# Moving a per-token middle stage into the window loop of a two-layer attention kernel, with the key split and the ones moved to other engines

## The reference, cut to what matters

```python
# layer 0: linear attention (ReLU features), mixed over tokens by a plain reshape
q, k, v = LN(x @ wq), LN(ctx @ wk), LN(ctx @ wv)
kv = einsum('bhnd,bhne->bhde', relu(k) + eps, v)
att = relu(q) @ kv / (relu(q) @ sum(k))
# the middle stage: all of it works on one token at a time
x = x + tanh(g_xattn[0]) * LN(att.reshape(B, -1, 128) @ dense_w + dense_b)
xq = round(LN(x) * 127 / max|LN(x)|)               # 8-bit rows, ternary weights
h = silu(xq @ w_gate) * (xq @ w_up)                # 128 -> 512
x = x + tanh(g_ffn[0]) * (round(h * 127 / max|h|) @ w_down)
q1 = LN(x) @ W_q                                   # queries of layer 1
# layer 1: softmax attention over the context, then 8 experts, 2 of them per token
s = softmax(q1 @ (ctx @ W_k).T / sqrt(8)) @ (ctx @ W_v)
x = x + tanh(g_xattn[1]) * (s @ W_o);  x = x + tanh(g_ffn[1]) * moe(LN(x))
```

## Time and profile before

| | us |
|---|---|
| time before, median of 3 runs | 834.42 (831.93 to 837.05) |
| the profiled execution, own time | 833.69 |
| its span | 831.8 |
| TensorE busy | 701.4 (84%) |
| VectorE busy | 563.2 (68%) |
| ScalarE busy | 482.8 (58%) |
| GpSimd busy | 252.7 (30%) |

### The profile page before, as it was taken

One profiled execution on the slowest core, in us unless ns is written; L12 is line 12 of the kernel. 1 busy time (PEld: TensorE's weight loads), 2 busy tenths in 40 slices (PEclk: granted clock), 3 DMA queues, 4 the chain that ended last, 5 costly groups with the idle time before them and its releaser, 6 DMA issues.

```text
span 831.8 us, 19578 instructions
## 1 busy us (share of the span) xinstructions
PE 701.4 (84%) x7276; PEld 485.1 (58%) x7277; DVE 563.2 (68%) x1099; ACT 482.8 (58%) x718; POOL 252.7 (30%) x236
## 2 busy tenths in 40 slices
PE   0599989985436489999999999999999999699997
PEld 0477767773313145666656666566665666467786
DVE  7699999984778767776767668676777775420111
ACT  0377777770324227667776777767777677344431
POOL 8198888880103522022210222112220110000000
PEclk9899999996657669999999999999999999699999
DMA  3022223344600071675446644466445561101110
GB/s 129 15 98 75 74 74 101 101 139 20 136 0 1 6 160 44 152 159 110 104 101 156 156 100 101 111 156 156 90 102 120 119 135 39 45 16 51 51 37 24
DMA packets 59460, 74.16 MB, mean 89 GB/s; under 512 B 35309, under 2 KB 40167, under 8 KB 59423
## 3 DMA queue, kind: packets, MB, share of 16 engines
q1 hardware_dynamic: 59422, 73.65, 37.3%
HBM read 32.61 MB, written 1.40 MB: 41 GB/s over the span
## 4 chain that ended last, share of the span: by engine, by line
PE 57%; DVE 24%; issue 10%; ACT 3%; DMA 1%; SPq 1%; POOL 1%; DVEq 1%; ACTq 0%
DVE mx L1227 8%; PE ps L605 7%; PE ps L496 7%; PE ps L663 6%; PE ps L675 6%; PE ps L488 6%; PE ps L592 6%; PE ps L482 5%; PE ps L431 3%; DVE ss L1029 3%; PE ps L445 2%; PE ps L517 2%; DVE xn L981 2%; ACT arena L735 2%; DVE arena L1049 2%
## 5 line engine op out<-in xcount | busy, mean ns | idle before, releaser
L1227 DVE TENSOR_REDUCE mx<-ps 128x1 f32<-128x500 f32 x336 | 214.3, 674 | 88.6 <-PE ps L496 87.4
L829 ACT ACTIVATE P<-ps,kbias,kscale 125x896 f32<-125x896 f32 x192 | 210.5, 1098 | 76.0 <-PE ps L592 71.7
L922 POOL TENSOR_TENSOR KP<-kvall,KP 128x1500 bf16<-128x1500 f32 x16 | 48.6, 3035 | 317.4 <-ACT KP L785 317.4
L496 PE MATMUL ps<-KP,Qb 128*128 128x500 bf16 x336 | 131.9, 394 | 9.8 <-issue 4.4
L605 PE MATMUL ps<-P,Vp 125*32 125x112 f32 x3072 | 113.4, 265 | 1.8 <-ACT P L829 1.3
L431 PE MATMUL ps<-wkv,cT 128*125 128x256 f32 x384 | 91.6, 382 | 1.2 <-ACT arena L748 1.2
L605 PEld LDWEIGHTS ps<-P,Vp 125*32 125x32 f32 x3072 | 67.1, 109 | 39.3 <-issue 31.5
L431 PEld LDWEIGHTS ps<-wkv,cT 128*125 128x125 f32 x384 | 69.1, 189 | 10.2 <-issue 1.5
L592 PEld LDWEIGHTS ps<-QS,KS 128*128 128x128 bf16 x768 | 53.9, 99 | 34.7 <-issue 18.5
L592 PE MATMUL ps<-QS,KS 128*128 128x112 bf16 x768 | 68.4, 214 | 5.7 <-DVE QS L1233 5.1
L592 PEld LDWEIGHTS ps<-QS,arena 128*128 128x128 bf16 x768 | 52.1, 98 | 33.3 <-issue 18.5
(11 more groups left out here) (190 smaller groups left out, 1000.6 us busy)
## 6 DMA issues: line engine op xcount, KB each, us to landing
cT<-ctxT_dram SPq DMA_DIRECT2D x32, 750.0 KB, 4.3
KS<-KP SPq DMA_DIRECT2D x48, 375.0 KB, 7.3
arena<-KP SPq DMA_DIRECT2D x48, 375.0 KB, 7.0
QS<-QD SPq DMA_DIRECT2D x96, 28.0 KB, 5.7
wgu<-w_dram SPq DMA_DIRECT2D x8, 256.0 KB, 2.8
...
```

The source lines that it names most:

```text
L496: ins = nc.tensor.matmul(ps[:, bank, 0:KCW], q[:, 128 * c:128 * c + 128], KP[par][0][:, KCW * k:KCW * k + KCW], start=True, stop=True)
L829: nc.scalar.activation(P[t % 2][0:TK, :].rearrange("p (k n) -> p k n", k=2), src, ACT.Exp, scale=kscale[0:TK, bass.ds(n, 1)], bias=kbias[0 ...
L1227: ins = v.tensor_reduce(mx[:, c, k:k + 1], ps[:, bank, 0:KCW], AX.X, ALU.max)
```

## The change

The middle stage no longer runs on all 8 tiles ahead of the windows. Tiles 0 and 1 still do, tile by tile; tile n = i+2 goes through it in the pair of windows i (windows 2i and 2i+1), for i = 0 to 5. Pairs 6 and 7 have no such work. Its products are ten new aux units (CHAIN): AT, DE (dense), XT, G (gate), U (up) in the first window of a pair, HT0, HT1, DN (down), LT, Q1 (query) in the second. PLACES becomes two tables. VectorE gets the per-tile steps between its maxima; GpSimd takes the inverse square roots (`deviation`: an add and a power of -0.5 on one column); SiLU is made of Tanh on ScalarE and a product on VectorE. Of the trip through DRAM, tiles 0 and 1 go first.

The key split: ScalarE writes the K unit in f32 to krest and frees the bank, then rounds krest to KP[0]; GpSimd subtracts KP[0] from krest; ScalarE rounds to KP[1] at the end of the window (t = 11; before t = 10); GpSimd makes KP[2] as before. `key_rest` is gone. The 1.0 in KS[0] and KS[1] are written by ScalarE (`fill_ones`, 6002 f32 that hold two bf16 ones each), at the very start and after the last step ahead of the windows.

```diff
-PLACES = [["MX0", "MX1", "V0"], ["MX2", "MX3", "MX4"], ["DEN", None, "V1"], ["MX5", "MX6", "V2"],
-          ["MX7", "WO", "K0"], ["MX8", "MX9", "MX10"], ["MX11", "MX12", "K1"], ["MX13", "MX14", "MX15"],
-          ["MX16", "MX17", "K2"], ["MX18", "MX19", "MX20"], [None, None, None], ["SH", None, None]]
-ALL = [u for places in PLACES for u in places if u]
+PLACES = [
+    [["MX0", "AT", "V0"], ["MX1", "MX2", "DE"], ["DEN", "MX3", "V1"], ["MX4", "MX5", "V2"],
+     ["MX6", "WO", "K0"], ["MX7", "MX8", "MX9"], ["MX10", "XT", "K1"], ["MX11", "MX12", "MX13"],
+     ["MX14", "MX15", "K2"], ["MX16", "MX17", "MX18"], ["MX19", "MX20", "G"], ["SH", None, "U"]],
+    [["MX0", "MX1", "V0"], ["MX2", "MX3", "MX4"], ["DEN", "HT0", "V1"], ["MX5", "HT1", "V2"],
+     ["MX6", "WO", "K0"], ["MX7", "DN", "MX8"], ["MX9", "MX10", "K1"], ["MX11", "MX12", "MX13"],
+     ["MX14", "LT", "K2"], ["MX15", "MX16", "MX17"], ["MX18", "MX19", "MX20"], ["SH", None, "Q1"]],
+]
+ALL = [[u for places in half for u in places if u] for half in PLACES]
 ENDS = ["DEN", "WO"]
-EARLY = ["K0", "K1", "K2", "V0", "V1", "V2", "K0'", "K1'", "K2'"]
-REST_LATER = 3
+CHAIN = ["AT", "DE", "XT", "G", "U", "HT0", "HT1", "DN", "LT", "Q1"]
...
+        KSF = [sb("KS0", [128, KSW // 2 + 1])[:], arena[:, 0:KSW // 2 + 1]]
+        KS = [k.bitcast(BF16)[:, 0:KSW] for k in KSF]
...
+            sp.wait_ge(sem("att0_ready"), 2)
+            mix_out(range(2, 5), "mix_out1")
+            sp.wait_ge(sem("mix_out0"), 64)
+            mix_in(slice(0, 2), "mix_in0")
+            mix_out(range(5, NT), "mix_out1")
+            sp.wait_ge(sem("mix_out1"), 32 * (NT - 2))
+            mix_in(slice(2, NT), "mix_in1")
...
+            for unit in EARLY_SIDE[0:3]:
+                fill(BEFORE, unit, 0, 0)
+            both("AT", "DE")
+            for unit in EARLY_SIDE[3:6]:
+                fill(BEFORE, unit, 0, 0)
+            both("XT", "G", "U")
+            fill(BEFORE, EARLY_SIDE[6], 1, 1)
+            both("HT0", "HT1", "DN")
+            fill(BEFORE, EARLY_SIDE[7], 1, 1)
+            both("LT")
+            fill(BEFORE, EARLY_SIDE[8], 1, 1)
+            both("Q1")
...
+            def fill_ones(n):
+                nc.scalar.copy(KSF[n], two_ones[:].broadcast_to([128, KSW // 2 + 1])).then_inc(sem(f"ks{n}_ready"), 1)
             act.wait_ge(sem("setup_done"), 1)
...
+            fill_ones(0)
...
+                if k == 0 and not (fixed(b) and b == 0):
+                    act.wait_ge(sem("kp3_ready"), b)
+                cols = slice(KCW * k, KCW * k + KCW)
+                nc.scalar.activation(krest[:, cols], ps[:, bank_of(at, unit), 0:KCW],
+                                     ACT.Identity, bias=bk_sb[:]).then_inc(sem("side_free"), 1)
+                act.wait_ge(sem("side_free"), emptied(at, unit))
+                nc.scalar.copy(KP[par][0][:, cols], krest[:, cols]).then_inc(sem("kp1_ready"), 1)
+            def key_part2(b, par):
+                act.wait_ge(sem("rest_ready"), b + 1)
                 nc.scalar.copy(KP[par][1][:], krest).then_inc(sem("kp2_ready"), 1)
...
+                elif unit == "G":
+                    act.wait_ge(sem("cg_ready"), n + 1)
+                    nc.scalar.activation(silu[:, z, :], ps[:, bank, :], ACT.Tanh,
+                                         scale=cg[:, z:z + 1]).then_inc(sem("tanh_ready"), 1)
...
+            key_part2(0, 0)
+            both("AT")
...
+            key_part2(1, 1)
+            act.wait_ge(sem("nd_ready"), 2)
+            fill_ones(1)
...
+                        if t == T - 1 and "K2" in has:
+                            key_part2(w + 2, par)
...
-                nc.gpsimd.memset(QS[n], 0.0)
-            nc.gpsimd.memset(KS[0], 1.0).then_inc(sem("zeroed"), 1)
...
+                pool.wait_ge(sem("kp1_ready"), KC * (b + 1))
+                nc.gpsimd.tensor_tensor(krest, krest, KP[par][0][:], ALU.subtract).then_inc(sem("rest_ready"), 1)
...
+            def deviation(n, j):
+                z = slot(n)
+                pool.wait_ge(sem("c_var"), turn(n, j, 3))
+                nc.gpsimd.tensor_tensor(sd[:, z:z + 1], mv[:, z, 1:2], (eps_ln if j else eps_in)[:], ALU.add).then_inc(sem("eps_added"), 1)
+                pool.wait_ge(sem("eps_added"), turn(n, j, 3))
+                nc.gpsimd.tensor_tensor(rstd[:, z:z + 1], sd[:, z:z + 1], mhalf[:], ALU.pow).then_inc(sem("rstd_ready"), 1)
...
-            nc.gpsimd.memset(KS[1], 1.0).then_inc(sem("ks1_ready"), 1)
...
+                    if par == 0 and chained:
+                        deviation(i + 2, 0)
+                        deviation(i + 2, 1)
+                    queries(b, par, i + 1, prev((i, par)))
+                    if par == 1 and chained:
+                        if not (fixed(i) and i == CHAIN_PAIRS - 1):
+                            mix_tile(i + 3)
+                        deviation(i + 2, 2)
...
+            def statistics(n, j, src):
+                z = slot(n)
+                v.bn_stats(stats[:, z, :], src).then_inc(sem("c_stat"), 1)
+                dve.wait_ge(sem("c_stat"), turn(n, j, 3))
+                pause()
+                v.bn_aggr(mv[:, z, :], stats[:, z, :]).then_inc(sem("c_var"), 1)
...
+            def dense(at, n):
+                z = slot(n)
+                name, = names(n, "DE")
+                src, free = opened(at, name)
+                v.tensor_tensor(lin[:, z, :], src, row[:, DENSE_B, :], ALU.add).then_inc(free, 1)
+                closed(at, name)
+                statistics(n, 0, lin[:, z, :])
+                dve.wait_ge(sem("c_var"), turn(n, 0, 3))
+                v.scalar_tensor_tensor(lin[:, z, :], lin[:, z, :], mv[:, z, 0:1], gmask[:], ALU.subtract,
+                                       ALU.mult).then_inc(sem("lin_ready"), 1)
...
+            def quantise(n):
+                z = slot(n)
+                dve.wait_ge(sem("rstd_ready"), turn(n, 1, 3))
+                v.tensor_scalar(nrm[:, z, :], x_of(n), mv[:, z, 0:1], rstd[:, z:z + 1], ALU.subtract,
+                                ALU.mult).then_inc(sem("n1_ready"), 1)
+                dve.wait_ge(sem("n1_ready"), n + 1)
+                row_steps(n, 0, nrm[:, z, :])
...
+            def gate(at, n):
+                z = slot(n)
+                name, = names(n, "G")
+                src, free = opened(at, name)
+                dve.wait_ge(sem("tanh_ready"), n + 1)
+                v.scalar_tensor_tensor(silu[:, z, :], silu[:, z, :], 1.0, src, ALU.add, ALU.mult).then_inc(free, 1)
...
+            def hidden_quantised(n):
+                z = slot(n)
+                dve.wait_ge(sem("qs_ready"), turn(n, 1, 2))
+                v.tensor_scalar(silu[:, z, :], silu[:, z, :], qs[:, z:z + 1], ROUND, ALU.mult,
+                                ALU.add).then_inc(sem("round_ready"), 1)
+                dve.wait_ge(sem("round_ready"), turn(n, 1, 2))
+                v.tensor_scalar(hqb[:, z, :], silu[:, z, :], ROUND, None, ALU.subtract).then_inc(sem("hq_ready"), 1)
+                v.tensor_scalar(cd[:, z:z + 1], cu[:, z:z + 1], wg2[:, 2:3], None,
+                                ALU.mult).then_inc(sem("cd_ready"), 1)
...
+                    elif unit == "DE":
+                        dense(at, n)
+                    elif unit == "G":
+                        gate(at, n)
+                    if chained:
+                        if unit == "MX5":
+                            first_sum(n)
+                        elif unit == "MX7":
+                            quantise(n)
+                        elif unit == "MX8":
+                            quantised(n)
...
+                if chained:
+                    hidden((i, 0), n)
...
+                        if unit == "MX0":
+                            hidden_steps((i, 0), n)
+                        elif unit == "MX1":
+                            hidden_quantised(n)
+                        elif unit == "MX10":
+                            normed(n)
```

742 lines of the change are left out of this document (429 added, 313 removed).

## The result

The changed kernel takes 857.55 us (median of 4 runs, 855.01 to 859.75) against 833.17 beside it (831.57 to 837.05). The ratio is 1.0286, 95% interval 1.0264 to 1.0308: slower, as forecast (850 us, range 808 to 864), and 7.5 us above the number. The profiled execution took 859.75 us (span 857.9), 26.1 more than the one of before; it is the longest of the four, and the clock differs among them (means of 0.914 to 0.930), so places where the clock falls are those of this execution.

The account below looks back on a forecast made before the run. Windows were taken as bound by TensorE's order, which waits for VectorE at a window's end. From 833.7 us, -6.5 (start), -41 (middle stage) and +63 (pairs) gave 849, stated as 850 against 834.4; range 808 to 864.

Parts of the forecast that it names:

- The start, -6.5: Kernel start: with the fill on ScalarE, the 8 normalisations run from 10.6 to 12.8, shifting everything behind by -6.5 us.
- The middle stage, -41: Between linear attention and first window: only 2 tiles go through ahead of the windows, -41 us, bounds -36 and -45.
- The hold that the forecast named as not isolated: Middle stage: dense's centring (L1348), with two SBUF inputs, would be held once by GpSimd reading SBUF, 1 us more.
- The first window, +5.0: First window of a pair: MX5, MX10 and XT wait for VectorE's steps, the gate for Tanh; +5.0 us.
- The second window, +2.7: Second window of a pair: hidden-row steps among MX0 to MX2 delay MX4, and the joint maximum comes late; +2.7 us.
- the port: Second window: VectorE's scaling and rounding wait for GpSimd's KP[2] and Qb; +2.7 us a pair, between 0 and 3.7.
- Rival 1: Pairs of windows: the port doesn't bite, a pair costs 7.7 us, total 833, no change; chance 0.24.
- Pair 0: First pair of windows: without DEN and WO it costs some 9 us, against 10.4 for a pair.
- its two bounds: Forecast's own range: port 1.5 to 3.7 us a pair, middle stage -36 to -45 us.
- Rival 3: Second windows: TensorE stands over 3 us at once, the clock falls, 2 to 3 us a pair more, 865; chance 0.12.
- Rival 2: Pairs: VectorE catches up, only TensorE's added products and the late gate stay, 4.3 us a pair, 812; chance 0.25.
- Rival 4: Windows: Tanh evicts Exp's table, two loads of 1.28 us a pair on ScalarE, 865; chance 0.01.

Follow-up runs that it names:

- e6: Changed kernel with GpSimd's KP[2] after the hidden rows' rounding, VectorE's quantisation one unit earlier and the gate's product at t = 8; 824.80 us, ratio 0.9897.
- e9: e6 plus Qb after the quantisation or rounding, KP[2] after Qb and On in the second window, dense's statistics behind MX3; 819.53 us, ratio 0.9828.
- e8: Changed kernel with 8 unread f32 products a pair that TensorE issues where it would wait; 847.39 us, ratio 1.0158.
- e1: Changed kernel, but in the first window's key part GpSimd starts KP[2] only after VectorE has scaled and rounded the hidden rows; 837.85 us, ratio 1.0047.
- e5: Changed kernel with the gate's product at t = 8, behind MX14, and MX15 to MX20 one or two places later; 862.36 us, ratio 1.0328.
- e3: Kernel before, with only the ones of both KS filled by ScalarE in place of GpSimd; 824.47 us, ratio 0.9892.
- e4: Kernel before, with only the key split: ScalarE writes f32 key rows and copies to bf16, GpSimd subtracts; 833.73 us, ratio 0.9998.

## Why the prediction was right, and where its numbers were off

**The start, -6.5: right, 1.4 short.** The step that failed is the table load behind the constants. There is one at 0.74, but it lies beside the setting of the constants, so the fill runs from 2.15 to 7.34 and not to 8.7. 5.19 us for 6002 elements is the rate taken from the 1500-element copy (5.3). By the Trainium skill (ScalarE: Activation LUTs, What ACT_TABLE_LOAD costs) a drain of some 1380 ns stands behind the load of a new set, and the forecast estimated a gain of 5.1 us from it. The rows show none: the load at 7.36 takes 1.28 and the square root runs at 8.65.

**The middle stage, -41: right.** First scores at 253.35 (forecast about 255). Of the -49.5, 7.2 had come by the products of L525 (L663 starts at 183.11 in place of 190.33), so the stage itself gave 42.3. AT is copied at 206.23; the forecast's 213.5 less 6.5 is 207.0. Qb ends at 235.9 and 238.6 (forecast 236.8). GpSimd's power had no row; it takes 0.55 for one column, the addition 0.19 to 0.24, so a root is 0.8 to 0.9 and not 0.6. The hold that the forecast named as not isolated is there: L1348 takes 1.32 beside KP[2] and 0.38 after it, 0.9 us. It has two inputs in SBUF. The Trainium skill (SBUF — State Buffer, Who interferes with whom) says that such an instruction contends with a GpSimd instruction that reads SBUF, and the trace agrees; L1509 in e6 (1.50 against 0.39 in e9) is a second case.

**The first window, +5.0: right at full clock.** Waits of 0.86, 0.91 and 0.84 us (forecast 1.05, 1.1 and 1.1) and of 1.65 in front of SH. e8 gives its length with the clock held up: 31.59 (forecast 31.25), +5.3. Windows without a fall in other runs agree: 31.67 in window 2 of after, 31.7 in window 4 of e1.

**The second window, +2.7 and +2.7 for the port: right, each 0.2 too dear.** The comparison is clean only at full clock. e6 without the hold: 28.76, +2.5. e8 with it: 31.27, so the port is 2.5 us. (e1's 29.18 has part of a fall in it; against that it would be 2.1.) At full clock the scaling took 1.74 (1.63 by the forecast), the rounding 1.79 (1.97); in after, where the second window starts at the lower clock, the scaling took 1.32. Rival 1, that the port doesn't bite, falls with these rows; e1 made it true and gave 837.9, near the 833 that this rival named, with the clock's falls still in it.

**The sum.** At full clock the middle pair takes 31.59 + 31.27 = 62.9, 10.4 over before, to the tenth what the forecast had; that it is the tenth is luck, since +0.3 in the first window and -0.2 twice in the second cancel. Pair 0 was priced at 9; in e8 it takes 62.2 against 51.6, so 10.7. Windows 12 to 14 cost 3.1 and not 2. With these the sum is 833.7 - 49.5 + 62.1 + 3.1 - 0.3 = 849, and e8, which is this with the clock kept up in the waits, took 847.4 (its first scores come 1 us sooner). That the sum is 849 again is luck in part too: 2.0 us were gained ahead of the windows and 2.2 lost in them. The forecast's own range of 843 to 858 is also narrower than its two bounds, which taken together give 839 to 861, and the measured 857.6 lies at its edge for a cause that was not in it.

**What failed is that the clock stood among the rivals and not in the sum.** Rival 3 said 2 to 3 us a pair and 865; it came at 1.8 (10.7 us over the six pairs) on top of all the rest, and that is the difference between 847 and 858. Its condition, a stand of over 3 us at once in a second window, held in one pair of six: in window 1 MX4 waited 3.31 us, and that window cost 2.7 us more than in e8, the price that the rival named. In e5 the stand was 3.2 to 3.3 us in every second window, and each lost 2.5 to 2.7 us against e8. But as a condition it was too narrow: in windows 4, 6 and 8 the clock fell behind two waits of 0.9 us in the first window of a pair. It was no alternative to the forecast but a surcharge on it, and each wait that the forecast derived should have carried it.

**Rival 2 (812, TensorE's own added work alone) was a statement about the placing.** In the kernel as it stood it was wrong. With six edits of order and of waits, e9 has pairs of 58.1, 5.6 over before, and is faster than before; the rival's point of decision was "under 6 us a pair". **Rival 4** is out: no table load stands in a window.

**What would make it pay.** The kernel as changed: -49.5 + 75.9 - 0.3 = +26.1. The ones by ScalarE, alone, are worth -9.5 (e3), the key split nothing (e4). The move of the middle stage is -42 + 76 in after, and in e9 (346.6 for windows 0 to 11 and 79.3 for 12 to 14, together 36.7 over before) -42 + 37. So the move itself gained some 5 us in the best of these kernels, which is also what lies between e9 and e3 (819.5 and 824.5).
